# Key sums of a linear attention made ahead of the first feed-forward, with the feature map on ScalarE and the head mask on GpSimd

## The reference

```python
def _feature_map(x):
    return jnp.where(x > 0, x + 1.0, jnp.exp(x))
...
kvp = kv @ Wkv.T
k, v = jnp.split(kvp, 2, axis=-1)
k = _feature_map(k.reshape(B, S, H, hd).transpose(0, 2, 1, 3))
v = v.reshape(B, S, H, hd).transpose(0, 2, 1, 3)
kv_summary = jnp.einsum('bhsd,bhse->bhde', k, v)
k_sum = k.sum(axis=-2)
z = 1.0 / (jnp.einsum('bhld,bhd->bhl', q, k_sum)[..., None] + EPS)
attn = jnp.einsum('bhld,bhde->bhle', q, kv_summary) * z
```

## Time and profile before

| | before |
|---|---|
| median of 3 runs | 521.31 us |
| span of the profiled execution | 517.5 us |
| TensorE busy | 449.8 us (87%) |
| VectorE busy | 360.9 us (70%) |
| ScalarE busy | 246.7 us (48%) |
| GpSimd busy | 154.5 us (30%) |
| first product of the first feed-forward (L636) | 43.42 us from the start |

### The profile page before, as it was taken

The page is one execution under the profiler, slowest core; times in us unless marked ns, Lnnn a source line. Parts: engine busy times, 40 slices in busy tenths (PEclk is TensorE's granted clock), DMA queues, the critical chain, the costliest instruction groups (busy, mean ns, idle before and its releaser), DMA issues. The chain is left out here.

```text
span 517.5 us, 7233 instructions
## 1 busy us (share of the span) xinstructions
PE 449.8 (87%) x2142; PEld 355.1 (69%) x2142; DVE 360.9 (70%) x1034; ACT 246.7 (48%) x452; POOL 154.5 (30%) x156
## 2 busy tenths in 40 slices
PE   1617999599999889999999999898999799899991
PEld 1315688368578666878778886787777588788851
DVE  6896779995289986565987966978867554531173
ACT  3618574363576346346125315470453454955540
POOL 3955342330002131110000001032336014477771
PEclk9966999799999989999999999999999999999997
DMA  8500312000300000960000000123232423346394
GB/s 303 187 31 30 103 31 83 0 1 0 101 2 0 2 0 14 310 178 0 1 1 1 1 0 2 32 71 102 90 115 83 123 73 91 114 139 208 85 385 153
DMA packets 32965, 42.00 MB, mean 81 GB/s; under 512 B 3483, under 2 KB 26781, under 8 KB 32928
## 3 DMA queue, kind: packets, MB, share of 16 engines
q1 hardware_dynamic: 28224, 32.28, 20.7%
q0 software_dynamic: 3744, 8.42, 4.4%
q10 hardware_dynamic: 960, 0.86, 0.5%
HBM read 24.97 MB, written 18.39 MB: 84 GB/s over the span
## 5 line engine op out<-in xcount | busy, mean ns | idle before, releaser
L660 PE MATMUL acc<-w_down,act_s 128*128 128x256 f32 x384 | 92.2, 387 | 0.9 <-DVE act_s L1386 0.9
L660 PEld LDWEIGHTS acc<-w_down,act_s 128*128 128x128 f32 x384 | 74.6, 195 | 13.2 <-DVE act_s L1386 1.3
L636 PE MATMUL ring<-xt_h,up_l 128*128 128x512 f32 x160 | 70.5, 441 | 2.9 <-DVE xt_l L1356 1.5
L1601 POOL TENSOR_TENSOR rstd<-var_eps,minus_half 128x4 f32<-128x4 f32 x14 | 14.9, 1068 | 176.5 <-DVE var_eps L1186 176.5
L637 PE MATMUL ring<-xt_l,up_h 128*128 128x512 f32 x160 | 63.8, 399 | 0.0
L638 PE MATMUL ring<-xt_h,up_h 128*128 128x512 f32 x160 | 63.7, 398 | 0.0
L1098 ACT ACTIVATE act_s<-ring 128x512 f32<-128x512 f32 x48 | 28.6, 597 | 59.9 <-PE ring L638 59.6
L631 PE MATMUL ring<-small,xn 128*128 128x128 f32 x160 | 23.6, 297 | 26.2 <-ACT xn L998 14.1
L699 PE MATMUL ring<-up_e,act_s 128*128 x184 | 44.3, 383 | 2.3 <-issue 2.0
L1637 POOL DMA_INDIRECT x_rows<-main_a,slots x32 | 31.1, 971 | 43.7 <-ACT main_a L1119 34.8
L1390 DVE TENSOR_TENSOR act_s<-ring,act_s 128x512 f32<-128x512 f32 x32 | 22.0, 686 | 30.8 <-PE ring L638 21.0
(11 more groups left out here) (275 smaller groups left out, 987.8 us busy)
## 6 DMA issues: line engine op xcount, KB each, us to landing
main_b<-x_rows SPq DMA_DIRECT2D x22, 257.0 KB, 2.8
x_rows<-v_t SPq DMA_DIRECT2D x1, 3983.5 KB, 16.7
up_l<-y_rows SPq DMA_DIRECT2D x5, 512.0 KB, 7.0
stage<-in_w_mlp SPq DMA_DIRECT2D x8, 256.0 KB, 2.6
up_e<-in_w_moe SPq DMA_DIRECT2D x8, 256.0 KB, 2.6
x_rows<-v_t SPq DMA_DIRECT2D x1, 1927.5 KB, 22.8
x_nat<-in_x SPq DMA_DIRECT2D x7, 256.0 KB, 7.7
out_x<-x_nat SPq DMA_DIRECT2D x6, 256.0 KB, 5.2
```

The source lines that it names most:

```text
L636: pe.matmul(out, wl, xh, start=first, stop=False, skip_group_check=True)
L660: last = pe.matmul(acc[t // 2][:, t % 2, :], act_s[n % RING][:, tok], w_down[:, u, :], start=u == 0 and t % 2 == 0, stop=final, skip_group ...
```

## The change

The entry `kv` is taken apart into five: `kv_k` (K on TensorE), `kv_e` (ScalarE's part of the feature map), `kv_v` (V on TensorE), `kv_c` (the sum copied from the bank by ScalarE) and `kv_m` (head mask by GpSimd, in place in `kv_sum`). VectorE has none of them. The feature map is now exp(-relu(-k)) + relu(k). ScalarE makes both terms (relu of -k, relu of k, values, then the exponential in place). For groups 0 and 1 the terms are not added: V is made by two products into the same bank, one of each term, so four products a sequence. For groups 2 and 3 GpSimd adds the terms and V stays two products. START now has the whole of group 0, and `kv_k 1 0` to `kv_k 1 2` with `kv_v 1 0`; one whole group and one sequence, that is five sequences with their sums before the first feed-forward (two K and one V of them were there before). In GpSimd's queue the addition of the past (`past_added`) moves one part forward and the second to fourth groups' `weigh_values` are spread over two parts. The first two `split` entries move back behind group 0's key sums.

```diff
-START = """wkv_in 0 0, setup 0 0, wkv_in 0 1, wkv_in 1 0, wkv_in 0 2, split 0 0, wkv_out 0 0, wkv_in 1 1, wkv_out 0 1, wkv_in 1 2,
...
+START = """wkv_in 0 0, setup 0 0, wkv_in 0 1, wkv_in 1 0, wkv_in 0 2, kv_k 0 0, kv_e 0 0, wkv_out 0 0, wkv_in 1 1, kv_k 0 1,
...
     ("mlp", 0): {
-        1: "wkv_out 1 5, casts 0 0",
-        2: "wkv_out 1 6 7, x_stats 1 0, kv 0 2",
...
+        1: "kv_v 1 1, wkv_out 1 5, casts 0 0, kv_e 1 2, kv_c 1 1",
+        2: "wkv_out 1 6 7, x_stats 1 0",
...
-        8: "peer_in 0 0, wkv_out 2 2 3",
-        9: "wkv_out 2 4 5, kv 1 0",
-        10: "wkv_out 2 6 7, x_stats 2 0, kv 1 1",
-        11: "mlp_in 1 0, kv 1 2",
-        12: "mlp_in 1 1",
...
+        8: "kv_k 1 3, kv_e 1 3, peer_in 0 0, kv_v 1 3, kv_c 1 3, wkv_out 2 2 3",
+        9: "wkv_out 2 4 5",
+        10: "wkv_out 2 6 7, x_stats 2 0, kv_m 0 0 1 2 3",
+        11: "mlp_in 1 0, kv_m 1 0 1",
+        12: "mlp_in 1 1, kv_m 1 2 3",
...
     ("mlp", 1): {
-        1: "mlp_out 0 0, kv 1 3 4, route 1 0, kv 2 0",
...
+        1: "mlp_out 0 0, route 1 0, kv_k 2 0, kv_e 2 0",
...
+OPEN_GROUPS = (0, 1)
...
+                elif kind == "kv_v":
+                    n = g * GT + part
                     once("pool_setup", pool_setup, 1)
...
+                    k_made(pe, n)
+                    key = (step, "V", part)
+                    bank = open_bank(key)
+                    keys = (k_e, k_r) if g in OPEN_GROUPS else (k_e,)
+                    for c in range(C):
+                        for m, rows in enumerate(keys):
...
-                    act.activation(k_e[n % 2][:, :], bank[:, 0:D], ACT.Exp)
+                    act.activation(k_e[n % 2][:, :], bank[:, 0:D], ACT.Relu, scale=-1.0).then_inc(k_negative, 1)
                     act.activation(k_r[n % 2][:, :], bank[:, 0:D], ACT.Relu)
                     act.activation(v_x[n % 2][:, :, 0:P], bank[:, D:].rearrange("p (c m) -> p c m", c=C),
-                                   ACT.Copy).then_inc(free_sem((step, "K", t)), 1)
+                                   ACT.Copy).then_inc(free_sem(key), 1)
+                    act.wait_ge(k_negative, n + 1)
+                    act.activation(k_e[n % 2][:, :], k_e[n % 2][:, :], ACT.Exp, scale=-1.0).then_inc(k_parts, 1)
+                elif kind == "kv_c":
+                    key = (("kv_v", g), "V", part)
+                    bank = full(act, key)
+                    act.activation(kv_sum[:, wkv_seqs(g)[part], :], bank[:, 0:C * KVW], ACT.Copy).then_inc(free_sem(key), 1)
...
+                elif kind == "kv_e" and g not in OPEN_GROUPS:
+                    n = g * GT + part
+                    pool.wait_ge(k_parts, n + 1)
+                    pool.tensor_tensor(k_e[n % 2][:, :], k_e[n % 2][:, :], k_r[n % 2][:, :], ALU.add).then_inc(k_ready, 1)
+                elif kind == "kv_m":
+                    if g == 0 and part == 0:
+                        pool.wait_ge(later_loaded, 16)
+                    freed(pool, (("kv_v", g), "V", part))
+                    rows = kv_sum[:, wkv_seqs(g)[part], :].rearrange("p (c m) -> p c m", c=C)
+                    pool.tensor_tensor(rows, rows, head_mask.unsqueeze(1).broadcast_to([P, C, KVW]),
+                                       ALU.mult).then_inc(kv_masked, 1)
```

More of the change, by code:

```diff
@@ L460, in build @@
         k_ready = sem("k_ready")
+        k_negative = sem("k_negative")
+        k_parts = sem("k_parts")
+        kv_masked = sem("kv_masked")
         diff_ready = sem("diff_ready")
@@ L525, in past_of, with k_made @@
             return ee_b_of[g][c][:, s, :].rearrange("p (t j) -> p t j", t=GT)[:, :, 0:P]
+        def k_made(eng, n):
+            opened = len(OPEN_GROUPS) * GT
+            eng.wait_ge(k_parts if n < opened else k_ready, n + 1 if n < opened else n + 1 - opened)
         def add_past(eng, g, c, s):
@@ L754, in _ @@
                     close_bank(key, last)
-                elif kind == "kv":
+                elif kind == "kv_k":
                     t = part
@@ L1601, in _ @@
                         pool.tensor_tensor(out, var_eps[:, n % 2, :], minus_half[:, :], ALU.pow).then_inc(rstd_ready, 1)
-                elif kind == "wkv_in" and part == 2:
-                    for c in range(g == 0, C):
-                        weigh_values(pool, g, c).then_inc(ev_ready, 1)
-                elif kind == "wkv_out" and part < 3:
+                elif kind == "wkv_in" and (part == 2 and g == 0 or part > 2):
+                    weigh_values(pool, g, C - 1 if g == 0 else part - 3).then_inc(ev_ready, 1)
+                elif kind == "kv_e" and g not in OPEN_GROUPS:
+                    n = g * GT + part
+                    pool.wait_ge(k_parts, n + 1)
[7 more added lines that the diff above has]
+                                       ALU.mult).then_inc(kv_masked, 1)
+                elif kind == "wkv_out" and part in (0, 1, 2, 4):
                     for c in range(C):
@@ L1610, in _ @@
                             pool.tensor_tensor(den, den, past_of(g, c, 1), ALU.add).then_inc(den_ready, 1)
+                    if part >= 2:
+                        c = part // 2 - 1
+                        y = by_token(ee_a[c][:, 0, :])
+                        pool.wait_ge(own_scaled, C * g + c + 1)
+                        pool.tensor_tensor(y, y, past_of(g, c, 0), ALU.add).then_inc(past_added, 1)
                 elif kind == "wkv_out" and part in (3, 5):
@@ L1699, in _ @@
                 step = (kind, g)
-                if step == ("kv", 0) and part == GT:
+                if step == ("kv_k", 0) and part == GT - 1:
                     sp.wait_ge(first_values, 1)
@@ L1704, in _ @@
                     load_ctx(2)
-                elif step == ("kv", 1) and part == GT:
+                elif step == ("kv_k", 1) and part == GT - 1:
                     sp.wait_ge(ev_ready, C * 2 - 1)
```

66 lines of the change are left out of this document (22 added, 44 removed), and 24 rows, old and new, of the table PLAN.

## The result

The changed kernel takes 515.94 us in the median of 4 runs (514.18 to 516.54), the kernel before beside it 520.77 (519.21 to 522.93): a ratio of 0.9897, 95% interval 0.9868 to 0.9927. That is a gain of 1.0%, where 2.7% was forecast (507.4 us). The profiled executions have spans of 517.5 and 514.0 us, 3.5 apart.

A forecast was written before the change was run, and what follows sets the result against it. The kernel was taken to be bound by TensorE's work plus the stretches in which it stands still. The terms 1.9 + 2.5 + 4.0 + 5.5 = 13.9 us came off 521.3, giving 507.4 us, range 502 to 516.

The forecast's parts named there:

- The opening: Before the first feed-forward: its first product starts near 39.1 us, 4.3 us earlier, through a shorter chain over ScalarE, VectorE and GpSimd.
- The new wait: First feed-forward's first units: TensorE stands 4.2 us at V(1,1) until ScalarE frees K(1,2)'s bank, with a low clock after.
- the first term: From the start to unit 3 of the first feed-forward: 1.9 us less, unit 3 starting at 62.7 instead of 64.25.
- First feed-forward's expert units: From unit 3 to the second feed-forward: 2.5 us less, mainly from operations taken off VectorE, which sets the pace there.
- second's first unit: Second feed-forward's first unit: K(1,3), V(1,2), a wait and V(1,3) all go, 4.0 us less.
- The masks' price: First feed-forward's expert units: GpSimd's eight masks could cost VectorE nothing to 6.4 us; 0.5 was taken.
- the last term: Second feed-forward's expert units: no wait for `exps_t_l` is left and TensorE keeps its clock, 5.5 us less.
- the key's longer path: Second feed-forward: table load, exponential and GpSimd's add take about 2.1 us more, covered by over 4 us of products.
- rival 4: Slower, chance 0.07: eleven V wait in TensorE's queue for ScalarE's exponential and GpSimd's add; up to +9 us, 530.
- The low clock after the old wait: Second feed-forward, after the wait of 3.82 us for `exps_t_l`: TensorE keeps its clock, saving 1.7 us.
- 2 (513): Rival, chance 0.23: GpSimd holds VectorE, the masks cost 6.4 us instead of 0.5; -8 us, 513.
- 3 (519): Rival, chance 0.14: little left; opening gains 0, V(1,1)'s wait costs 2.4, masks cost 6.4 us; -2 us, 519.

## Why the prediction was wrong

*The opening* (forecast 4.3 us to unit 0, measured 2.84). The chain was the right one and every engine did what was said of it; the sizes were too kind. Group 0's last product is done 1.36 us earlier, not 1.9: the reciprocals end at 25.10, but GpSimd's L1635 starts at 27.12, behind a value product of group 1 (L525) that took 2.12 us. The normalization starts at 35.38, not 34.4, and the step from its end to the first product takes 3.13 us, not 2.7.

*The new wait.* V(1,1) was named, its cause too: 3.63 us against 4.2, by ScalarE's copy into `v_x`. That unit 1 ends 15.6 us after the normalization came out at 15.2.

*The step that failed in the first term* is the stretch from group 1's residual to unit 3, priced at 10.2 us. It took 12.24 (53.63 to 65.87). I took 1.17 us off the old 11.4 for a product that is ready now, and left the rest alone. But two K and three V had stood in that stretch, one V is left, and I had counted them only as work saved. The transposes do come sooner after the residual, by 0.86 us (7.11 against 7.97). But TensorE now idles 3.34 us ahead of them instead of 0.48, and then works at a low clock:

```profile
60.00:66.00 6.00, 4.37 (x13) 2.45 (x13) 2.54 (x12) 1.19 (x2) 1.01 (x1) 0.61 0.20 66
```

In the kernel before, transposes and routing product read

```profile
60.82 1.09 PE L631 MATMUL ring<-small,xn 128*128 128x128 f32 x8 [0.48 <-DVE xn L1201]
...
62.86 1.96 PE L785 MATMUL ring<-main_b,later 128*128 128x512 f32 x4 [0.47 <-ACT main_b L1033]
```

From the start of the routing product to unit 3 it took 1.39 us before and takes 2.76 now, twice as long; from the transposes to unit 3 it took 3.43 us, with a V in between, and takes 5.13 without. So 2.04 of the term's 3.5 us were lost here. Of the rest, 1.05 is the opening (the normalization ends at 37.45, not 36.4) and 0.35 I had rounded in, from 1.55 to 1.9. The same is seen at 110.22, where transposes take 1.97 us after a wait of 4.59, instead of 1.09.

*First feed-forward's expert units, second's first unit.* 2.0 and 4.0 us, where 2.5 and 4.0 were forecast. The masks' price of 0.5 us was at most 0.25. A reading behind it was wrong: by the earlier trace rows four scans lost 1.84 us beside GpSimd, 0.46 each, not 0.9.

*The step that failed in the last term* is "`exps_t_l` is ready 2.2 us earlier, TensorE reaches it 3.8 later: no wait is left". The first part is right: it is ready at 179.94 instead of 182.34. But TensorE does not reach it, as it stands at V(3,0). I had priced the key's longer path at 2.1 us of work and covered it by a unit of products; I had not walked GpSimd's queue, in which the add stands behind a product that waits 6 us for VectorE. This is rival 4's kind of wait at one place, with a length that rival 4 didn't have: not the key's path, but what stands ahead of it. Of the 7.0 us missed, the two moved adds gave back 4.44. The other 2.6 are mine as well. 1.86 us of standing still are left when both adds are early, 1.25 of it the wait for `exps_t_l`, where I had put none. The low clock after the old wait I priced at 1.7 us from PEclk over 5 us, while the same 338 products take 73.49 us busy in the kernel before and 72.54 with no fall: 0.95.

*The forecast's whole* of 13.9 us was not absurd: with the two waits removed, the same method and nearly the same order give 12.2. But the forecast had counted the wait at V(1,1) in, so that the two sums lie near each other is partly luck. *The rivals*: the amounts of 2 (513) and 3 (519) both lie 3 us from the result, nearer than mine, and neither by its reasons. The masks cost at most 0.25 us instead of 6.4, which refutes 2; for 3 the opening would have had to gain nothing, and it gained 2.84. Only its +2.4 for the first term came near the measured +1.62.

## What to carry to other kernels

When an operation moves to another engine, walk that engine's queue at the new place: what stands ahead of it, and what that waits for, sets when its result comes, not its own duration. And ask at each place whether the operation has to move there: in the window of V(3,0) the run that left it on VectorE was the fastest. Work taken out of a wait is no gain there, and may cost: it leaves TensorE idle, and the products behind it run slower. Filler has to be looked at on every engine: a K that TensorE does for nothing brought ScalarE two table loads in front of a silu. And a change of method and of order together is not the sum of the two; here each alone was slower than the kernel before.

## What the runs showed of the hardware

- The same wait does not always cost the same: the low clock after it lasts longer in some executions. After V(3,0) had waited 4.33 or 4.34 us, the way from that feed-forward's unit 8 to unit 10 took 14.25, 14.32, 15.04, 15.68, 15.76 and 15.76 us in six profiles with the same instructions in that stretch, at a mean granted clock of 0.93 in the first and 0.83 in the last two; it took 14.84 where V did not wait and 1.25 us were waited later. With the block stretch (7.8 us, or 9.3 to 10.2), the two places account for 3 us between runs.
- A normalization of four tiles on VectorE took 1.38 us alone and 3.20 beside GpSimd's masks, while reciprocals of 128x256 beside GpSimd kept 1.69 to 1.75. The Trainium skill, SBUF — State Buffer, "Who interferes with whom", lets an operation with one SBUF input contend with GpSimd only in a mode with two ports; the rows agree in so far as the two operations behave differently.
- A scan pair took 2.36 us alone and 3.96 beside two GpSimd products, which took 2.08 and 2.19 instead of 1.27: both sides paid.
